# One block of a vision tower on one core: the start-up order of tile 0, a bank for tile 2's tokens, and the last store in halves

## The reference

```python
x5 = concat([x] + four_shifts(x)); tokens = patchify(x5, 16)       # 64 tokens of 3840 per image
h = layernorm(tokens) * gamma + beta;  h = h @ W + b               # width 192
q, k, v = heads(layernorm(h) @ w_qkv.T)                            # 12 heads of 16
k1 = k2 = k3 = softmax(q @ k.T)      # 64 tokens = 64 landmarks, so the three kernels are one matrix
V = K.T / max(sum(K))                # iterative inverse, 6 steps:
V = 0.25 * V @ (13 I - KV @ (15 I - KV @ (7 I - KV)))
h = h + (k1 @ inverse(k2) @ (k3 @ v)) @ w_proj.T + b_proj
p = softmax(layernorm(h) @ router.T); keep the top 8 of 16 experts, normalised
h = h + sum_e comb[e] * gelu(layernorm(h) @ w1[e]) @ w2[e]         # widths 8 x 128, 8 x 256
```

## Time and profile before

| | |
|---|---|
| median of 3 runs | 694.73 us (694.63 to 696.47) |
| profiled execution, its own time | 698.12 us |
| its span, first to last instruction | 696.3 us |
| mean granted TensorE clock in the span | 0.992 |
| busy in the span: PE, DVE, ACT, POOL | 654.2, 495.9, 385.6, 105.1 us |

### The profile page before, as it was taken

The page is one execution under the profiler, slowest core; times in us unless marked ns, Lnnn a source line. Parts: engine busy times, 40 slices in busy tenths (PEclk is TensorE's granted clock), DMA queues, the critical chain, the costliest instruction groups (busy, mean ns, idle before and its releaser), DMA issues.

```text
span 696.3 us, 29941 instructions
## 1 busy us (share of the span) xinstructions
PE 654.2 (94%) x13218; PEld 571.8 (82%) x13218; DVE 495.9 (71%) x1351; ACT 385.6 (55%) x1045; POOL 105.1 (15%) x328
## 2 busy tenths in 40 slices
PE   4678999999999999999999998899999999999997
PEld 2467788888888888888888787688999999999996
DVE  5457878878878888888888986576456547556643
ACT  0126666766776766676676766744444444333332
POOL 1302023123123222312312400110000000000000
PEclk9979999999999999999999999999999999999999
DMA  8792111121121121111100000000000000000000
GB/s 310 269 268 88 34 49 49 34 63 34 34 64 35 35 64 35 41 56 35 34 4 5 4 4 4 5 0 2 0 24 1 1 0 24 2 1 23 1 1 23
DMA packets 13409, 30.64 MB, mean 44 GB/s; under 512 B 1248, under 2 KB 7520, under 8 KB 13024
## 3 DMA queue, kind: packets, MB, share of 16 engines
q1 hardware_dynamic: 13280, 28.73, 12.7%
HBM read 27.16 MB, written 1.57 MB: 41 GB/s over the span
## 4 chain that ended last, share of the span: by engine, by line
PE 86%; DVE 5%; ACT 3%; issue 1%; DVEq 0%
PE ps L400 29%; PE ps L566 18%; PE ps L556 16%; PE ps L289 5%; PE ps L306 2%; PE ps L367 2%; PE ps L418 2%; PE ps L349 2%; PE ps L307 2%; DVE uu L848 1%; PE ps L341 1%; DVE se L804 1%; DVE sst L802 1%; PE ps L431 1%; PE ps L321 1%
## 5 line engine op out<-in xcount | busy, mean ns | idle before, releaser
L907 DVE SCALAR_TENSOR_TENSOR acc<-ps,comb,acc 128x192 f32<-128x192 f32 x256 | 89.1, 411 | 84.6 <-PE ps L566 84.5
L566 PE MATMUL ps<-w_sb,work 128*128 128x192 f32 x768 | 140.3, 326 | 0.7 <-ACT work L735 0.7
L566 PEld LDWEIGHTS ps<-w_sb,work 128*128 128x128 f32 x768 | 129.3, 189 | 9.0 <-issue 1.1
L735 ACT ACTIVATE work<-ps 128x512 f32<-128x512 f32 x96 | 57.3, 597 | 138.6 <-PE ps L556 138.6
L400 PEld LDWEIGHTS ps<-rr 64*64 64x64 f32 x3840 | 97.3, 134 | 20.9 <-issue 12.6
L400 PE MATMUL ps<-rr 64*64 64x64 f32 x3840 | 109.9, 222 | 4.4 <-issue 3.5
L848 DVE SCALAR_TENSOR_TENSOR uu<-rr,qq 128x384 f32<-128x384 f32 x160 | 86.3, 562 | 32.3 <-ACT qq L641 25.0
L400 PE MATMUL ps<-uu,qq 64*64 64x64 f32 x4608 | 98.4, 225 | 11.1 <-DVE uu L848 10.7
L400 PEld LDWEIGHTS ps<-uu,qq 64*64 64x64 f32 x4608 | 82.1, 134 | 28.0 <-DVE uu L848 18.4
L648 ACT ACTIVATE rr<-ps 128x384 f32<-128x384 f32 x160 | 73.7, 489 | 55.4 <-PE ps L400 54.7
L645 ACT ACTIVATE qq<-ps 128x384 f32<-128x384 f32 x96 | 47.1, 490 | 8.7 <-PE ps L400 3.1
(11 more groups left out here) (142 smaller groups left out, 1072.2 us busy)
## 6 DMA issues: line engine op xcount, KB each, us to landing
xtb<-xt_dram SPq DMA_DIRECT2D x16, 512.0 KB, 3.5
work<-x_dram SPq DMA_DIRECT2D x16, 512.0 KB, 4.0
wsh<-ws_dram SPq DMA_DIRECT2D x10, 288.0 KB, 5.6
w_sb<-w_dram SPq DMA_DIRECT2D x1, 2304.0 KB, 20.8
w_a<-w_dram SPq DMA_DIRECT2D x1, 1536.0 KB, 7.3
w_b<-w_dram SPq DMA_DIRECT2D x2, 768.0 KB, 11.9
out_dram<-acc SPq DMA_DIRECT2D x4, 384.0 KB, 2.6
mult<-copies_dram SPq DMA_DIRECT2D x1, 512.0 KB, 8.5
```

Source lines behind the costliest of these rows:

```text
L566: last = pe.matmul(ps[:, 2 + 2 * (e % 2) + j // 2, (j % 2) * DIM:(j % 2 + 1) * DIM], hid[:, n % 4, j * P:(j + 1) * P], w2_sb[:, c, :], sta ...
L735: act.activation(hid[:, n % 4, :], ps[:, UPB[n % 3], :], ACT.Gelu_apprx_tanh).then_inc(gelu_done, 1)
L907: last = dve.scalar_tensor_tensor(out=a, in0=ps[:, 2 + 2 * (e % 2) + j // 2, (j % 2) * DIM:(j % 2 + 1) * DIM], scalar=comb[:, g * GT + j, ...
```

## The change

There are five edits.

1. VectorE's prologue: `less_max(0)` moves ahead of `hidden(1)`, `softmax_scale(0)` ahead of `normed(1)`, and `token_sums(2)` from the end of the prologue to behind `normed(1)`, ahead of the column sums.
2. TensorE's prologue: `tok(2)` moves right behind `scores(0)`, `transpose_kernel(0)` ahead of `transpose_xl(1)`, and `qk(1)` behind `spread_denominators(0)`. ScalarE's follows: `copy_kernel(0)` ahead of `copy_xl(1)`, and `save_y(0)` ahead of `copy_q(1)`.
3. `value(1)` and its copy leave the prologue for the first window of step 0 of iteration 0.
4. `tok(2)` writes bank 2 in place of C. Its waits for `t1_ready` and `v_copied` go; Newton's first use of lane 1 waits for `t1_ready` 3.
5. The last expert of the last group: TensorE signals behind the second tile's matmuls of the last chunk and again behind the fourth's. `add_expert` adds two tiles, signals, waits and adds the other two, and SP stores the last four tiles as two DMAs of 192 KB.

```diff
--- before.py
+++ after.py
@@ -128,6 +128,9 @@
         ps = ctx.enter_context(nc.psum_tensor("ps", [P, 8, 512], F32))
         A, B, C, D = (ps[:, i, :] for i in (4, 5, 6, 7))
 
+
+        def tok_bank(t):
+            return ps[:, 2, :] if t == 2 else C
 
         def sums_bank(t):
             return ps[:, 3, :] if t == 0 else D
@@ -205,11 +208,17 @@
             sp.dma_start(w2_sb[:], w2.rearrange("(c p) n -> p c n", p=P)).then_inc(ffw_loaded, 16)
             for t in range(4, NT):
                 tile_loads(t)
-            for g in range(NT // GT):
+            def store(t0, t1):
+                sp.dma_start(out[t0:t1].rearrange("t p n -> p t n"), acc[:, t0:t1, :]).then_inc(out_stored, 16)
+
+            for g in range(NT // GT - 1):
                 sp.wait_ge(expert_added, (g + 1) * EXPERTS + 2)
-                sp.dma_start(out[g * GT:(g + 1) * GT].rearrange("t p n -> p t n"),
-                             acc[:, g * GT:(g + 1) * GT, :]).then_inc(out_stored, 16)
-            sp.wait_ge(out_stored, 16 * (NT // GT))
+                store(g * GT, (g + 1) * GT)
+            sp.wait_ge(expert_added, NT // GT * EXPERTS + 2)
+            store(NT - GT, NT - 2)
+            sp.wait_ge(expert_added, NT // GT * EXPERTS + 3)
+            store(NT - 2, NT)
+            sp.wait_ge(out_stored, 16 * (NT // GT + 1))
 
 
         @block.gpsimd
@@ -279,14 +288,12 @@
             def tok(t, c0, c1):
                 if c0 == 0:
                     pe.wait_ge(xt_loaded[t % 2], 16 * (t // 2 + 1))
-                    if t >= 1:
+                    if t == 1:
                         pe.wait_ge(t1_ready, t)
-                    if t == 2:
-                        pe.wait_ge(v_copied, 2)
                     if t >= 3:
                         pe.wait_ge(sdiff, 2 * t - 3)
                 for c in range(c0, c1):
-                    last = pe.matmul(C[:, 0:DIM + 1], xtb[:, t % 2, c, :], weff[:, c, :], start=(c == 0), stop=(c == CH - 1))
+                    last = pe.matmul(tok_bank(t)[:, 0:DIM + 1], xtb[:, t % 2, c, :], weff[:, c, :], start=(c == 0), stop=(c == CH - 1))
                 if c1 == CH:
                     last.then_inc(tok_done, 1)
 
@@ -388,6 +395,8 @@
                     pe.wait_ge(r_ready, n - 1)
                 else:
                     pe.wait_ge(r0_ready, 2 * t + lane + 1)
+                    if t == 0 and lane == 1:
+                        pe.wait_ge(t1_ready, 3)
                     if t >= 1:
                         pe.wait_ge(r_ready, n - 1)
                 lhs, rhs = (src, src) if phase == 0 else (qq, uu)
@@ -432,7 +441,7 @@
                 last.then_inc(logits_done, 1)
 
             def first_window(k, t):
-                if k == 0 and on(t + 1) and t >= 1:
+                if k == 0 and on(t + 1):
                     value(t + 1)
                 if k == 1 and on(t - 1):
                     out_heads(t - 1)
@@ -525,14 +534,13 @@
             qk(0)
             value(0)
             scores(0)
+            tok(2, 0, CH)
+            transpose_kernel(0)
             transpose_xl(1)
-            qk(1)
-            transpose_kernel(0)
             transpose_sums(0)
             gram(0)
-            value(1)
             spread_denominators(0)
-            tok(2, 0, CH)
+            qk(1)
             for t in range(0, NT):
                 iteration(t)
 
@@ -567,6 +575,8 @@
                                      hid[:, n % 4, j * P:(j + 1) * P], w2_sb[:, c, :],
                                      start=(c == FIRST[e] and j % 2 == 0), stop=(c == FIRST[e] + WIDTH[e] - 1),
                                      skip_group_check=True)
+                    if n == NC - 1 and j == 1:
+                        last.then_inc(down_done, 1)
                 if c == FIRST[e] + WIDTH[e] - 1:
                     last.then_inc(down_done, 1)
 
@@ -719,11 +729,10 @@
             copy_q(0)
             copy_value(0)
             exponents(0)
+            copy_kernel(0)
             copy_xl(1)
+            save_y(0)
             copy_q(1)
-            copy_kernel(0)
-            copy_value(1)
-            save_y(0)
             for t in range(0, NT):
                 iteration(t)
 
@@ -750,13 +759,13 @@
         def _(dve):
             def token_mean(t):
                 dve.wait_ge(tok_done, t + 1)
-                dve.tensor_scalar(st[:, 0:1], C[:, DIM:DIM + 1], -1.0, None, ALU.mult).then_inc(mu_ready, 1)
+                dve.tensor_scalar(st[:, 0:1], tok_bank(t)[:, DIM:DIM + 1], -1.0, None, ALU.mult).then_inc(mu_ready, 1)
 
             def token_sums(t):
                 if t > 0:
                     token_mean(t)
                 dve.wait_ge(mu_ready, t + 1)
-                dve.scalar_tensor_tensor(out=t1[:], in0=wsum[:], scalar=st[:, 0:1], in1=C[:, 0:DIM],
+                dve.scalar_tensor_tensor(out=t1[:], in0=wsum[:], scalar=st[:, 0:1], in1=tok_bank(t)[:, 0:DIM],
                                          op0=ALU.mult, op1=ALU.add).then_inc(t1_ready, 1)
 
             def variance(t):
@@ -899,10 +908,13 @@
                     dve.tensor_tensor(w[r, k, :], raw[r, col:col + P], high[r, k, :].bitcast(F32),
                                       ALU.subtract).then_inc(wlo_ready, 1)
 
-            def add_expert(g, e):
+            def add_expert(g, e, n):
                 dve.wait_ge(down_done, g * EXPERTS + e + 1)
                 dve.wait_ge(expert_added, g * EXPERTS + e + 2)
                 for j in range(GT):
+                    if n == NC - 1 and j == 2:
+                        last.then_inc(expert_added, 1)
+                        dve.wait_ge(down_done, g * EXPERTS + e + 2)
                     a = acc[:, g * GT + j, :]
                     last = dve.scalar_tensor_tensor(
                         out=a, in0=ps[:, 2 + 2 * (e % 2) + j // 2, (j % 2) * DIM:(j % 2 + 1) * DIM],
@@ -1000,10 +1012,11 @@
             token_sums(1)
             variance(1)
             masked_keys(0)
+            less_max(0)
             hidden(1)
-            less_max(0)
+            softmax_scale(0)
             normed(1)
-            softmax_scale(0)
+            token_sums(2)
             dve.wait_ge(kt_done, 2)
             column_sums(0, B, 4, 2, colsum_b)
             dve.wait_ge(kt_copied, 1)
@@ -1011,7 +1024,6 @@
             denominators(0)
             start_newton(0)
             masked_keys(1)
-            token_sums(2)
             for t in range(0, NT):
                 iteration(t)
 
@@ -1034,7 +1046,7 @@
                 g, c = divmod(n, HID)
                 e = EXPERT_OF[c]
                 if c == FIRST[e] + WIDTH[e] - 1:
-                    add_expert(g, e)
+                    add_expert(g, e, n)
 
 
 def kernel(x, L0_tok_gamma, L0_tok_beta, L0_tok_W, L0_tok_b, L0_attn_w_qkv, L0_attn_w_proj, L0_attn_b_proj,
```

## The result

| | before | after |
|---|---|---|
| median | 694.73 us (694.21 to 696.47, 5 runs) | 691.82 us (691.05 to 694.64, 5 runs) |
| ratio, 95% interval | | 0.9952 (0.9933 to 0.997) |
| profiled execution, its span | 698.12, 696.3 | 694.64, 692.8 |
| mean granted clock in it | 0.992 | 0.988 |

The kernel became 2.9 us faster; 691.2 was forecast. Two later sets of runs gave ratios of 0.9963 (0.9948 to 0.9979) and 0.9951 (0.9938 to 0.9964), so 2.4 to 4.0 us less. On the profiled executions' own scale the gain is 3.5 us, and there 7.1 was forecast. So the total came out right and a large term of its working did not.

What follows compares the result with a forecast made beforehand. TensorE carries 86% of the chain, so gains lie only where it idles or runs at low clock. 6.05-0.2+1.25 = 7.1 gives 691.0 on the profile's scale; 694.73-3.4 = 691.3 on the median's. Predicted 691.2, range 690.0 to 692.5.

Steps and rivals of the forecast that it cites:

- the bridge: From profiled execution to median: before's low clock is missing in most timed runs, so 3.7 of the 7.1 us gain drops out.
- VectorE's new order: Prologue: tile 0's maximum starts at 32.62 right behind the scores; its softmax multiply ends at 38.09, where it was 39.29.
- The new wait at normed(1): VectorE's prologue: GpSimd, held up beside the softmax multiply, delays normed(1) by 0.6 us; normed(1) itself then takes 0.71.
- tok(2) and the transposes: TensorE's prologue: tok(2) fills idle time from 32.6 to 35.5; transposes start at 38.1, taking 0.9 us at full clock.
- No low clock in the changed kernel: The kernel after has no low-clock stretch in profile or timed runs; some 3.5 us of the gain ahead of Newton is clock.
- Rival B: Clock falls in TensorE's new 2.6 us gap, 35.5 to 38.1: +2.9 us, 694.1, the same as before; chance 0.12.
- No low clock in two of the three timed runs before: Two timed runs of the kernel before had no fall ahead of Newton, the one at 696.47 part of it.
- rival A: The timed runs contain the low clock, so all 7.1 us comes off the median: 687.6; chance 0.14.
- value(1) in the window: Step 0 of iteration 0: value(1) between the two phases costs 0.2 us, bounds 0 and 0.85.
- The code comes late (C): TensorE's code is late at Newton's start while DMA engines carry FFN weights: +1.6 us, 692.8; chance 0.12.
- the sign of 1 us: TensorE idle for "issue" above 1 us in 44 to 55 us of the profile after would show code coming late.
- The last sum and store: Kernel's end: first sums start 0.65 us earlier, the smaller last store saves 0.6; 1.25 us gained.

Runs made afterwards that it cites:

- all the fills: Changed kernel plus added unread matmuls in four idle places of TensorE: ratio 0.9945; the same with normed(1) behind the column sums and tile 2's token sums later: 0.9933.
- end_only: The kernel before with only edit 5, the last sum and store in halves: 693.20 us against 694.91, ratio 0.9979.
- kernels with fills: Kernels with added TensorE matmuls whose result nobody reads; on the changed kernel, ten behind tok(2) gave ratio 0.9947, four idle places 0.9945.
- spread_w: Changed kernel with the 6 MB of FFN weights as ten DMAs behind the loads of tiles 5 to 14: 700.26 us, ratio 1.0084 to the kernel before.
- after_third: The changed kernel run a third time, unaltered, beside the kernel before: 691.00 us against 695.02, ratio 0.9951.
- tok_late: Changed kernel with tile 2's tokens and their sums back at the prologue's end, still in bank 2: 693.57 us, ratio 0.9993 to the kernel before.

## Why the prediction was right, and where it was wrong

The total is right by luck as much as by its working. On the profiled executions' scale the gain was 3.5 us and not 7.1, and the bridge from there to the medians was 0.6 (the profile lay 3.4 above the median before and 2.8 after) and not 3.7. The two misses, 3.6 and 3.1, have opposite signs.

- *VectorE's new order:* right. The softmax ended 0.6 earlier than forecast on the clock of the trace, but the scores came 0.36 earlier too.
- *The new wait at normed(1):* right in mechanism and size, 0.64 and 0.76 for 0.6 and 0.71. The row of tile 1 in iteration 0 carried it. By the Trainium skill (GPSIMD Engine Reference, 8. Key points) GpSimd contends with VectorE instructions of two SBUF inputs. The trace agrees: 0.81 for 0.19 beside the multiply.
- *tok(2) and the transposes:* tok(2) right (32.13 to 35.02). The transposes started right behind the multiply and took 1.54, not 0.9. (The prediction's 1.29 for half clock is from the chain's row; the timeline of before has 1.49 for them, at 40.94.)
- *No low clock in the changed kernel:* wrong, and this is the step that failed. "Both scales agree, because the kernel after has no low stretch in either" assumed that 2.5 us of idleness are too short for a fall. It fell at 37.35, before the idleness ended, and stood low twice more (23.7 to 27.1 and 54.4 to 61.2). Over the 23 executions of the changed kernel the mean granted clock lay between 0.988 and 0.995, which is 7 us or more at half clock in each. Rival B named this, but not as the rule. The kernels with all the fills show the forecast chain where the clock stays, and there its working holds: 11.66 us for 11.83, and 2.5 for the order. B's price was too high as well: 1.2 us, not 2.9, since the clock was back at 44.2, ahead of the last qk matmuls, and 2.0 in the other profiles.
- *No low clock in two of the three timed runs before:* wrong too. Over 77 executions of before in the three sets the mean granted clock lay between 0.989 and 0.995: each has 7 to 15 us at half clock, what lies behind the last matmul included. So rival A was right that the timed runs contain the fall, and wrong in its 687.6, because the changed kernel contains it as well. The 3.4 us between profile and median were not its amount of low clock, since the profiled execution has the usual 0.992: before's executions spread from 691.3 to 698.3, and the profiled one was a slow one. Its fall lay on the chain (Newton at 50.50), where end_only's lay mostly in idle time (47.85); how much of the 3.4 that is stays open.
- *value(1) in the window:* right, 0.2. From Newton's first squares to its first products it is 2.35 us, and was 2.16.
- *The code comes late (C):* happened too, in a smaller size than its 1.6. TensorE's stalls between 44 and 55 us were 0.68 and 0.46, together 1.14, which passes the sign of 1 us that the prediction set for C. A second profile has 0.70, the third none, three kernels with fills 1.1 to 2.7. All end 1.3 to 1.6 us after an instruction packet has landed (see spread_w).
- *The last sum and store:* right, 1.27 for 1.25, and 1.25 again with that edit alone.
- *What remains open:* in the profiles of all kernels but spread_w the stretch from Newton's first matmul to the last one varies from 637.9 to 644.5 us, and not with the order. Falls and stalls are part of it; I have no account for all of it. The changed kernel's profile had 644.5, before's 641.3, which is why 5.4 us at Newton's start and 1.27 at the end became 3.5.

## What to carry to other kernels

One profiled execution is one draw: before its low-clock stretch is priced into a sum, compare its time with the spread of many runs, and expect the same idle hole to be hit elsewhere next time. Where TensorE waits a few microseconds in a start-up chain, matmuls into a part of a bank that nobody reads are a one-line test of what the clock costs there; here they were worth nearly as much as the reorder. Look whether a small GpSimd chain moves beside a large VectorE instruction with two SBUF inputs: here one instruction of it ended only 0.05 us behind the VectorE one, and a VectorE instruction queued for the chain held all that followed. And a stall without a releaser can be set beside the packets of the "instruction" queue before it is called unexplained.

## What the hardware showed unasked

- In the changed kernel the clock fell at 54.4, half a microsecond behind a wait of 1.89 us that ended at 53.92, with TensorE busy between. In the kernel before the same wait, up to 58.41, brought no fall, nor did it in after_third (up to 53.62). Rival B of the prediction took 0.54 us as the longest idle time that the clock had outlasted; this row of before was a nearer one.
- The low stretches ahead of the last matmul were 3.4 to 13.7 us long (the longest in tok_late, 33.2 to 46.8). Behind the scores the clock fell 1.0 us into TensorE's idle time in tok_late, 2.3 in the changed kernel's first profile (there behind tile 2's tokens) and 4.2 in before, and in after_third 2.5 us of it passed without a fall. So the length of an idle time alone didn't tell whether the clock would fall in it.
- TensorE's code has a rhythm that can be seen: a packet of 16 KB every 3.1 us or more, and a stall when one is late.
- Starting earlier can meet a queue: with Newton at 43.6, TensorE stood 2.5 us without a releaser in the second step, while the DMA engines moved the weights at a share of 1.0; the instruction packet landed at 49.53 and TensorE resumed at 51.01. With Newton at 50.5, and at 45.6 in after_third, it did not.
